# A gated MoE and MLP kernel: the token index stored behind each row, and the first expert steps in another order

## What is computed

```python
# experts: context ctx[e] is gate, up and down weight of expert e (4 experts, 512 x 512)
expert_ids = minimum(clip(token_ids, 0, 24999) // 6250, 3)
g = silu(einsum('bsd,fd->bsf', h, ctx[e])); u = einsum('bsd,fd->bsf', h, ctx[e])
y = einsum('bsf,df->bsd', g * u, ctx[e])            # for the tokens with expert_ids == e
x = x + tanh(g_xattn[0]) * y                        # h = layernorm(x)
# dense MLP, 1408 inner features, ternary weights with scales
g = einsum('th,ih->ti', xf, gate_w) * gate_s;  u = einsum('th,ih->ti', xf, up_w) * up_s
x = x + tanh(g_ffn[0]) * (einsum('ti,hi->th', silu(g) * u, down_w) * down_s)   # xf = layernorm(x)
```

## Time and profile before

| | |
|---|---|
| time of the runs, median | 388.78 us |
| profiled execution | 389.44 us, of which the span is 387.7 us |
| TensorE busy | 373.1 us (96%) |
| VectorE busy | 243.5 us (63%) |
| ScalarE busy | 147.1 us (38%) |
| GpSimd busy | 81.8 us (21%) |
| context load, `ctx_in<-ctxT` | 4 transfers of 1024 KB |
| granted clock of TensorE, mean | 0.994 |

### The profile page before, as it was taken

How to read it: one execution, slowest core, us unless ns; L and a number is a source line. 1 busy time by engine, 2 the same in 40 slices (tenths; PEclk the granted TensorE clock), 3 DMA queues, 4 the chain that set the end, 5 groups by cost and what they waited for, 6 DMA issues and landing times.

```text
span 387.7 us, 5617 instructions
## 1 busy us (share of the span) xinstructions
PE 373.1 (96%) x1757; PEld 303.1 (78%) x1757; DVE 243.5 (63%) x455; ACT 147.1 (38%) x265; POOL 81.8 (21%) x108
## 2 busy tenths in 40 slices
PE   3999999999999999999999999999999999999992
PEld 2477788888888878888888888888888888888891
DVE  6888856667877678778847255747246757222253
ACT  4355556565545346422332223332222332222220
POOL 7523443434352120010002101002101001200011
PEclk9999999999999999999999999999999999999997
DMA  6775666663221126333201322200232300100011
GB/s 221 258 253 191 248 216 253 210 216 102 89 68 68 56 86 216 97 119 81 83 0 54 135 80 83 71 11 31 88 124 62 101 27 27 81 0 0 0 41 73
DMA packets 21905, 40.91 MB, mean 106 GB/s; under 512 B 2672, under 2 KB 8816, under 8 KB 21888
## 3 DMA queue, kind: packets, MB, share of 16 engines
q1 hardware_dynamic: 17536, 26.50, 21.3%
q0 software_dynamic: 4352, 14.19, 9.8%
HBM read 28.36 MB, written 12.32 MB: 105 GB/s over the span
## 4 chain that ended last, share of the span: by engine, by line
PE 93%; DVE 3%; POOL 1%; issue 1%; ACT 0%; DVEq 0%; POOLq 0%
PE bank L1149 40%; PE bank L1045 26%; PE bank L1156 20%; PE bank L1031 2%; PE bank L1060 2%; PE bank L1073 1%; POOL minus_j L362 1%; PE bank L1021 0%; DVE rows L934 0%; PE bank L1012 0%; DVE tmp L927 0%; DVE xn L927 0%; DVE is_low L647 0%; PE bank L1083 0%; DVE sh L882 0%
## 5 line engine op out<-in xcount | busy, mean ns | idle before, releaser
L1149 PE MATMUL bank<-work,wgu 128*128 (+1 forms) x736 | 167.3, 380 | 0.0
L1149 PEld LDWEIGHTS bank<-work,wgu 128*128 128x128 f32 x736 | 133.9, 188 | 27.1 <-issue 0.5
L1045 PE MATMUL bank<-work,parts 128*128 (+1 forms) x432 | 110.7, 402 | 0.8 <-ACT parts L463 0.2
L1045 PEld LDWEIGHTS bank<-work,parts 128*128 128x128 f32 x432 | 78.5, 188 | 20.0 <-issue 2.9
L1156 PE MATMUL bank<-work,hp 128*128 128x512 f32 x352 | 87.2, 390 | 0.2 <-DVE hp L886 0.2
L1156 PEld LDWEIGHTS bank<-work,hp 128*128 128x128 f32 x352 | 65.7, 188 | 14.4 <-DVE hp L886 0.6
L867 DVE SCALAR_TENSOR_TENSOR sh<-bank,gs,sh 128x512 f32<-128x512 f32 x42 | 31.5, 749 | 55.6 <-PE bank L1149 55.6
L567 ACT ACTIVATE hp<-sh 128x512 fp32r<-128x512 f32 x42 | 26.6, 634 | 78.7 <-DVE sh L867 78.7
L562 ACT ACTIVATE sh<-bank,gs 128x512 f32<-128x512 f32 x42 | 28.9, 689 | 71.6 <-PE bank L1149 68.8
L391 POOL TENSOR_TENSOR rstd<-ve,half 128x1 f32<-128x1 f32 x31 | 18.1, 583 | 124.3 <-DVE ve L708 124.3
L446 POOL DMA_INDIRECT out<-rows,oidx x16 | 16.2, 1011 | 128.0 <-DVE rows L934 105.8
(11 more groups left out here) (132 smaller groups left out, 267.4 us busy)
## 6 DMA issues: line engine op xcount, KB each, us to landing
wraw<-guT SPq DMA_DIRECT2D x8, 704.0 KB
ctx_in<-ctxT SPq DMA_DIRECT2D x4, 1024.0 KB, 6.1
rows<-x_rows SPq DMA_DIRECT2D x8, 512.0 KB, 4.4
turned_rows<-xn SPq DMA_DIRECT2D x12, 256.0 KB, 2.7
rows<-turned_rows SPq DMA_DIRECT2D x12, 256.0 KB, 2.7
checked<-dwT SPq DMA_DIRECT2D x11, 256.0 KB
rows<-dwT SPq DMA_DIRECT2D x11, 256.0 KB, 2.9
rows<-x,gidx POOLq DMA_INDIRECT x19
```

The source lines that it names most:

```text
L1045: mm = pe.matmul(out_ps[:, :], part(s)[:, c * P:(c + 1) * P], ctx_w(e, c, w), start=n == 0, stop=n == last)
L1149: mm = pe.matmul(out_ps[:, tiles.start * P:tiles.stop * P], wgu[:, row + h, w, c * P:(c + 1) * P], moving, start=n == 0, stop=n == last)
```

## The change

**The output table goes.** The ring of rows becomes 16 words wider (`WIDE`, 528 words for 512), and so does the scratch tensor. Behind each gathered row GpSimd writes the token's index (`token_in`, a copy from `gidx`), the store takes the whole wide row along, the MLP's loads bring it back, and the last write to `out` takes its indices from behind the rows (`token_of`). The operations that made `oidx` are gone: on VectorE rounding, `is_low` anew, `is_high`, `in_tile` and a cast, on TensorE 16 matmuls. A memset clears the 16 words of the ring's six slots once.

**Seven low parts of the context on GpSimd.** Those in `ON_POOL`; the other nine stay on VectorE. TensorE waits for the one or the other count (`ctx_low_ready`).

**Tile 0 in halves.** `norm`, transposes, `x_hi` and `x_lo` of tile 0 work on 256 columns at a time, the two halves in two PSUM banks. 11 fill-ins stand ahead and 2 behind.

The diff, with edits left out that only cut a row to its first 512 words:

```diff
+WIDE = D + 16
...
+ON_POOL = [(1, 2), (1, 3), (2, 0), (2, 1), (2, 2), (3, 0), (3, 1)]
+ON_VECTOR = [(e, c) for e in range(EXPERTS) for c in range(KC) if (e, c) not in ON_POOL]
+HALF = D // 2
...
-    scratch = nc.dram_tensor("x1_rows", [2 * TOKENS + STEPS * P, D], F32).ap()
+    scratch = nc.dram_tensor("x1_rows", [2 * TOKENS + STEPS * P, WIDE], F32).ap()
...
-        rows = sb("rows", [P, ROWS, D], F32)
+        rows = sb("rows", [P, ROWS, WIDE], F32)
...
-        oidx = sb("oidx", [P, TILES], U32)
...
+        def token_of(first, last):
+
+            return rows[:, first:last, D:D + 1].bitcast(U32)
+
+        def first_xt(i):
+
+            return (xt_ps, ht_ps)[i][:, i * HALF:(i + 1) * HALF]
+
...
-            sp.wait_ge(S["ctx_lo"], EXPERTS * KC)
+            sp.wait_ge(S["ctx_lo"], len(ON_VECTOR))
+            sp.wait_ge(S["pool_ctx_lo"], len(ON_POOL))
...
+            def ctx_lo(n_from, n_to):
+                for n in range(n_from, n_to):
+                    e, c = ON_POOL[n]
+                    pool.wait_ge(S["ctx_hi"], KC * e + c + 1)
+                    pool.tensor_tensor(ctx_w(e, c, 1), ctx_in[:, e, c, :], ctx_w(e, c, 0).bitcast(F32),
+                                       ALU.subtract).then_inc(S["pool_ctx_lo"], 1)
+
+            def token_in(k, count=1):
+                at = ring_slot(k)
+                pool.tensor_copy(token_of(at, at + count), gidx[:, k:k + count].unsqueeze(2))\
+                    .then_inc(S["token_in"], count)
...
+            pool.memset(rows[:, 0:RING, D:WIDE], 0.0).then_inc(S["pads"], 1)
...
             inverse_std(0)
             gather(2)
             gather(3)
+            pool.wait_ge(S["pads"], 1)
+            token_in(0, 2)
+            token_in(2, 4)
             inverse_std(1)
+            pool.wait_ge(S["xn_ready"], 2)
+            ctx_lo(0, 2)
+            inverse_std(2)
             gather(4)
-            inverse_std(2)
+            pool.wait_ge(S["xn_ready"], 3)
+            ctx_lo(2, 5)
+            inverse_std(3)
             pool.wait_ge(S["early_row"], 16)
             gather(5)
-            inverse_std(3)
-            pool.wait_ge(S["tables_ready"], 2)
+            pool.wait_ge(S["token_in"], 6)
+            pool.wait_ge(S["tables_ready"], 3)
             pool.wait_ge(S["rows_ready"], 1)
             store(0)
+            ctx_lo(5, 7)
             for k in range(2, STEPS + 1):
                 if k + 2 < STEPS:
                     inverse_std(k + 2)
@@ -425,10 +462,10 @@
                 pool.wait_ge(S["stored"], 16 * (k - 1))
                 if k + 4 < STEPS:
                     gather(k + 4)
+                    token_in(k + 4)
+                pool.wait_ge(S["token_in"], k)
                 pool.wait_ge(S["rows_ready"], k)
                 store(k - 1)
-
-            pool.wait_ge(S["oidx_ready"], 1)
 
             for b in range(BLOCKS):
                 if b + 1 < BLOCKS:
@@ -444,8 +481,8 @@
                     else:
                         done = last_stored[t]
                     pool.indirect_dma_start(
-                        out, bass.IndirectOffsetOnAxis(ap=oidx[:, BLOCK * b + t:BLOCK * b + t + 1], axis=0),
-                        rows[:, row_slot(b, t), :], None).then_inc(done, 16)
+                        out, bass.IndirectOffsetOnAxis(ap=token_of(row_slot(b, t), row_slot(b, t) + 1)[:, 0, :], axis=0),
+                        rows[:, row_slot(b, t), 0:D], None).then_inc(done, 16)
...
             ctx_hi(0)
             ctx_hi(1)
-            x_hi(0)
+            for i, (done, ready) in enumerate((("xt_half", "xhi_half"), ("xt_done", "xhi_ready"))):
+                act.wait_ge(S[done], 1)
+                act.activation(tile_x(0)[:, i * HALF:(i + 1) * HALF], first_xt(i), ACT.Copy)\
+                   .then_inc(S[ready], 1)
             ctx_hi(2, range(0, 2))
             silu(0)
             x_hi(1)
...
-            def over_out(a):
-                return a[:, :].unsqueeze(1).to_broadcast([P, TILES, CT])
-
-            then(dve.tensor_scalar(tile_up[:, :], rank[:, :], -(P - 1) / 2, ROUND, ALU.add, ALU.add))
-            dve.scalar_tensor_tensor(out=minus_low[:, :], in0=tile_up[:, :], scalar=ROUND,
-                                     in1=rank[:, :], op0=ALU.subtract, op1=ALU.subtract)
-            then(dve.tensor_scalar(high[:, :], tile_up[:, :], -ROUND, None, ALU.add))
+            def ctx_lo(n_from, n_to):
+                for e, c in ON_VECTOR[n_from:n_to]:
+                    dve.wait_ge(S["ctx_hi"], KC * e + c + 1)
+                    dve.tensor_tensor(ctx_w(e, c, 1), ctx_in[:, e, c, :], ctx_w(e, c, 0).bitcast(F32),
+                                      ALU.subtract).then_inc(S["ctx_lo"], 1)
+
+            ctx_lo(0, 1)
             of_slot = bank[5][:, 0:2 * STEPS]
             dve.wait_ge(S["route_pe"], 4)
             dve.tensor_copy(gidx[:, 1:STEPS], of_slot[:, 1:STEPS]).then_inc(S["tables_ready"], 1)
-            is_out = is_high[:, 0:TILES, :]
-            dve.tensor_tensor(is_low[:, :, :], minus_low[:, :].unsqueeze(1).to_broadcast([P, P, CT]),
-                              minus_j[:, :, :], ALU.is_equal).then_inc(S["low_ready"], 1)
-            then(dve.tensor_tensor(is_out, over_out(high), tile_of[:, 0:TILES, :], ALU.is_equal))
-            dve.tensor_copy(tiles[:, :, :], owner[:, 2:4, :])
-            dve.tensor_tensor(in_tile[:, 0, 0:TILES, :], is_out, over_out(token), ALU.mult)\
-               .then_inc(S["route_sb"], 1)
-
-            def index_tables():
-                dve.wait_ge(S["route_sb"], 4)
-                for i in range(2):
-                    dve.tensor_tensor(shifted[:, i, :], tiles[:, 0, 1 - i:1 - i + PACKED], shifts[:, :],
-                                      ALU.logical_shift_left)
+            then(dve.tensor_copy(tiles[:, :, :], owner[:, 2:4, :]))
+            for i in range(2):
+                shift = dve.tensor_tensor(shifted[:, i, :], tiles[:, 0, 1 - i:1 - i + PACKED], shifts[:, :],
+                                          ALU.logical_shift_left)
+            then(shift)
+            dve.tensor_reduce(packed[:, :], shifted[:, :, :], AX, ALU.bitwise_xor).then_inc(S["tables_ready"], 1)
+            ctx_lo(1, 3)
+
+            def store_table():
                 then(dve.scalar_tensor_tensor(out=empty[:, :], in0=of_slot[:, STEPS:], scalar=0.0,
                                               in1=dump[:, :], op0=ALU.is_equal, op1=ALU.mult))
                 dve.scalar_tensor_tensor(out=sidx[:, :], in0=empty[:, :], scalar=-1.0,
                                          in1=of_slot[:, STEPS:], op0=ALU.add, op1=ALU.add)\
                    .then_inc(S["tables_ready"], 1)
-                dve.tensor_reduce(packed[:, :], shifted[:, :, :], AX, ALU.bitwise_xor)\
-                   .then_inc(S["tables_ready"], 1)
...
-            def step_with_ctx(k):
-                ctx_lo(KC * k, KC * (k + 1))
-                norm(k + 1, ring_slot(k + 1))
-                h_lo(k - 1)
-                hidden(k)
-                x_lo(k + 1)
-                landed(k + 2)
-                stats(k + 2, ring_slot(k + 2))
-                if k == 1:
-                    dve.wait_ge(S["gates_ready"], 1)
-                update(k - 1)
+            def first_x_halves():
+
+                dve.wait_ge(S["rstd_ready"], 1)
+                for i, ready in enumerate(("first_half", "xn_ready")):
+                    part = slice(i * HALF, (i + 1) * HALF)
+                    dve.tensor_scalar(xn[:, part], rows[:, ring_slot(0), part], mv[:, 0, 0:1], rstd[:, 0:1],
+                                      ALU.subtract, ALU.mult).then_inc(S[ready], 1)
+
+            def first_x_low_halves():
+                for i, ready in enumerate(("xhi_half", "xhi_ready")):
+                    part = slice(i * HALF, (i + 1) * HALF)
+                    dve.wait_ge(S[ready], 1)
+                    low = dve.tensor_tensor(tile_x(1)[:, part], first_xt(i), tile_x(0)[:, part].bitcast(F32),
+                                            ALU.subtract)
+                low.then_inc(S["xlo_ready"], 1)
 
             landed(0)
             stats(0, ring_slot(0))
-            ctx_lo(0, 1)
-            norm(0, ring_slot(0))
-            index_tables()
-            ctx_lo(1, 2)
-            x_lo(0)
+            store_table()
+            first_x_halves()
+            ctx_lo(3, 4)
+            first_x_low_halves()
+            ctx_lo(4, 5)
             landed(1)
             stats(1, ring_slot(1))
-            ctx_lo(2, KC)
             norm(1, ring_slot(1))
             hidden(0)
             landed(2)
             stats(2, ring_slot(2))
             x_lo(1)
-            for k in range(1, EXPERTS):
-                step_with_ctx(k)
-            dve.wait_ge(S["route_pe"], 5)
-            dve.tensor_copy(oidx[:, :], bank[4][:, 0:TILES]).then_inc(S["oidx_ready"], 1)
+            ctx_lo(5, 6)
+            norm(2, ring_slot(2))
+            h_lo(0)
+            hidden(1)
+            x_lo(2)
+            landed(3)
+            stats(3, ring_slot(3))
```

(41 more changed lines are left out.)

64 lines of the change are left out of this document (35 added, 29 removed).

## The result

The changed kernel took **385.87 us** (385.25 to 387.91, 6 runs) against 388.88 us for the kernel before (388.47 to 389.75, 6 runs): ratio 0.9932, interval [0.9915, 0.9949]. The forecast was 386.0 us. The profiled execution took 385.9 us with a span of 384.2 us (389.44 and 387.7 before).

What follows compares the result with a forecast made beforehand. TensorE's own work, plus its waits for VectorE's low parts, was taken as the bound. Gains of 1.33 + 0.91 + 0.69 = 2.93 us, less 0.1 for the memset, give 2.8 and 386.0 us; own range 385.5 to 386.5, 8-in-10 range 385.1 to 387.6.

Steps and rivals of the forecast that it cites:

- The bound: Whole kernel: TensorE's own work is 93% of the span; VectorE's low parts cost the first three steps 2.37 us.
- Table matmuls worth nothing: Behind product 0: removing 16 output-table matmuls (1.19 us) gains nothing, as the turn waits for silu and hidden product anyway.
- Rival B: Fewer fill-ins delay TensorE's clock rise past product 0's start: some 1.3 us lost, 387.3 us, chance 0.08.
- Tile 0: First tile in halves: statistics at 12.3, normalising at about 14.15, first matmul at 15.5 to 15.6 us instead of 16.49.
- Stop behind the context transfer: ScalarE ahead of product 1: silu of tile 0 waits behind two context copies until 19.1; product 1 starts at 21.2, not 22.43.
- Product 2, the term of 1.33 us: Third product starts at 28.3 for 29.63 us, held by VectorE waiting half a microsecond for tile 2's rows.
- rival A: Tile 2's gather lands sooner, so product 1 runs through and its turn comes 0.7 us earlier: 385.3 us, chance 0.13.
- Steps 2 and 3: Expert steps behind product 2 run at the 6.43 us floor, gaining 0.91 and 0.69 us.
- GpSimd's price: A low part of 512 columns on GpSimd takes 1.2 us (0.62 to 1.85), free up to 1.67.
- Rest of the program: From 44 us on all moves with TensorE; index copy hidden; at the MLP's start silu has about 1 us to spare.
- two of its own signs of being wrong: Wrong if product 4 is not about 2.8 us early, or if that lead shrinks between 50 us and the end.
- Rival E: Transfers set the pace later, by cut rows or fixed arrivals: whole 2.8 us given back, 388.8; chance 0.05, 0.02 more for slower.

Runs made afterwards that it cites:

- e2: Changed kernel with GpSimd's seven low parts back on VectorE, so all sixteen there: median 388.74 us, ratio 0.9998 to the kernel before.
- e1: Kernel before the change with only the output table replaced by the token index behind each row: median 388.1 us, ratio 0.9983.
- e3: Changed kernel with tile 0 as one piece of 512 columns instead of halves: median 386.28 us, ratio 0.9919 to the kernel before.
- e5: Changed kernel with TensorE's two loads of the experts' numbers moved ahead of tile 1's transposes: median 385.67 us.
- e9: Changed kernel with six more fill-in matmuls on TensorE, three ahead of tile 1's turn and three behind it: median 385.50 us.
- e12: The changed kernel itself again, on one chip beside its variants with fill-ins: median 386.62 us, ratio 0.9951 to the kernel before.
- e11: Changed kernel with six fill-ins, down rows spread 2, 3, 3, 3, experts' number loads ahead of tile 1's turn, and earlier silu of tile 0: median 385.26 us.
- e7: Changed kernel with down rows' parts spread over the first MLP chunks as 2, 3, 3, 3 instead of 3, 3, 3, 2: median 385.45 us.
- e4: Changed kernel with each of GpSimd's seven low parts made twice: median 394.12 us, ratio 1.0135 to the kernel before.
- e6: Changed kernel with the fourth context matrix asked for only when tile 2's rows have landed: median 387.06 us.
- e8: Changed kernel with early experts' number loads, late fourth context, down rows spread 2, 3, 3, 3, and silu of tile 0 ahead of two context copies: median 385.63 us.

## Why the prediction was right, and where it was off

- **The bound.** Right in the main: most of the gain is TensorE's waits in the first steps. e2 shows that the low parts of VectorE held them. Not all of it: half a microsecond lies behind them, in the steady steps (see the sum).
- **Table matmuls worth nothing.** Right for the first steps (e1: product 4 at 44.03 for 44.09). But e1's edit as a whole, priced at nothing, brings some 0.5 us by the end. Incomplete as well: the matmuls kept TensorE busy in a stretch where it now has 1.3 us of work, and the clock may fall behind it. Rival B saw the clock as a risk ahead of product 0, where no run showed it; it came behind it.
- **Tile 0.** Forecast 15.5 to 15.6, measured 15.20. The step that was too long is the work ahead of the statistics: they started at 11.93 rather than 12.3, so the extra low parts cost nothing, and normalising started at 13.82 rather than 14.15. From there to the first matmul it took 1.38 us, as forecast (1.35 to 1.45). e3 gives the halves 0.43 us at product 4.
- **Stop behind the context transfer.** Right in kind: silu came behind the two high parts, at 18.52 (forecast 19.1), since the transfer landed 0.4 us sooner than in the profile before. Of this 0.6 us only 0.2 reached product 1 (20.98, forecast 21.2), for a term that was missing: the two loads of the experts' numbers on TensorE's sequencer, which keep the turn 0.75 us behind the hidden product (e5).
- **Product 2, the term of 1.33 us.** It came out at 1.93. VectorE did wait for tile 2's rows, 0.48 us, but they landed at 20.3 and not 20.94: rival A, in part (0.64 of its 0.7 us). A part of this is luck of the profiled execution, since the landing moves by itself: where VectorE waited for it in other profiles, the statistics started at 20.41 (e9), 20.44 (e12), 20.66 (e2, e11) and 20.99 (e7), and e7's product 2 started at 28.36, where the forecast had it.
- **Steps 2 and 3, 0.91 + 0.69.** Measured 0.94 and 0.70: 7.34 us became 6.40, and 7.12 became 6.42.
- **GpSimd's price.** 1.31 us at the median of seven (1.27 to 1.32) for 1.2 taken, inside the free margin. The Trainium skill (GPSIMD Engine Reference, 3.1 Elementwise) leads to the estimate of 1.1, a sixth low. The same page of the Trainium skill also warns of contention with VectorE's operations of two inputs in SBUF (8. Key points); here VectorE's low parts took 0.757 us at most for a median of 0.684, and the deviations 0.587 at most, where the kernel before had two of 0.94 and 0.958. e4 had low parts of 1.61 and 1.62 us among others of 1.26 to 1.31, and VectorE's low parts beside them took 1.01 and 0.81. So the contention is there, but in the changed kernel it was small, and off the path.
- **Rest of the program.** This is where it failed, and two of its own signs of being wrong came true: product 4 was 3.57 us early and not about 2.8, and the lead shrank between 50 us and the end, from 4.02 to 2.81. "Behind it silu has about 1 us to spare" took the stores as they were; with a store some 1.6 us slower (its successor waited 4.17 us, and 2.58 where the store was not met) ScalarE waited 2.28 us instead of 0.38, and 1.21 us came back. Rival E had the mechanism (transfers that set the pace later), at 2.8 us lost, for another reason. The wide rows are not the cause: e1 stores them too and loses nothing there. Nor is a row cut into a long and a short piece: a store has 80 packets in both kernels, 16 of them under 512 bytes.
- **The sum.** 1.93 + 0.94 + 0.70 = 3.57 at product 4, then 0.45 more over fifteen steps (6.40 for 6.43 us each; e1 has 0.39 of it, so most of it comes with e1's edit), less 1.21 at the MLP: 2.81, with 2.8 forecast. The total was right by luck: two misses cancelled. The lead up to the MLP was 1.19 us more than forecast (0.64 at product 4, mostly the earlier landing, 0.45 behind it, and 0.1 for the memset, which put the gather of tile 0 back by 0.08, from 8.36 to 8.44, but no product), and the 1.21 us lost at the MLP were not forecast. Without the second it would have been near 384.7 by this sum, which is an estimate and below the range given; e7, whose profile has no such loss, measured 385.45. And the median itself moves: on the chip of e12 the changed kernel took 386.62 against 388.70, a gain of 2.1 us and not 3.0.

## What to carry to other kernels

When an engine is relieved of work that "lay in a wait anyway", look at what the work may have done besides: here TensorE was left with a gap behind which its clock fell in some executions. A lead won early has to be followed through every change of stage, and the slack there is not to be taken from one profile: the wait for the store ahead was 3.5 us in the kernel before, and 2.6 to 4.4 us in its variants. A single load on one engine that everybody waits for (here one down row in the first chunk) is cheaper to move back a chunk than to hurry.

## What the runs showed of the hardware

- TensorE's granted clock fell to 0.50 (the 1.2 GHz level) for 3.41 us in three of the profiled executions (e5, e6 and e4, starting at 21.50, 21.71 and 21.43; in e4 again at 35.08, behind 0.82 us of work in the 3.08 us before it), each time behind the stretch from 18 to 21 us in which it had been busy 1.25, 1.20 and 1.07 us. Six other executions with this gap kept 1.00: the changed kernel's own (1.29 us busy) and e2, e3, e7, e8 and e12 (1.39 to 1.72).
- The start of the clock's full level differed between executions of the same code: 12.35 us in the changed kernel, 15.05 in e7, which differs from it only in the MLP.
- An instruction load of one 16 KB packet took 0.88 to 2.02 us on one DMA engine; in eight of the fourteen profiles it fell among a store's packets, and the wait for that store was 4.0 to 4.4 us in seven of them and 3.5 us in the kernel before, instead of 2.6 to 2.7.
- GpSimd copied one token index per row in 0.18 to 0.75 us, nearly all of it hidden in its wait for the store's landing: four of its stores waited for a copy, 0.7 us in all.
- Beside a low part on GpSimd, VectorE's low parts took up to 1.01 us (e4) for a median of 0.685.
